# Image keys of batches 3 to 10 of a cross-attention: two batches at a time, by seven products for eight blocks, with the context sums on VectorE

## The chip, the core and the metric

The kernel runs on one core of a Trainium2 chip. The metric is the device time of one execution in microseconds (us); lower is better. Engines are named as the profile names them: PE is TensorE (PEld its weight loads), DVE is VectorE, ACT is ScalarE, POOL is GpSimd, SP is SyncE. ACT and SP also issue DMAs.

## The reference

Input `x` is 16 batches of 512 tokens by 640 channels, the context `ctx_2048` 16 batches of 512 tokens by 1024 channels. Context tokens 0 to 76 are text, then come 4 object and 4 other tokens, and 427 image tokens. Cut to what matters (`heads` splits 640 channels into 20 heads of 32):

```python
q = heads(x @ to_q_w)
h_txt = sdpa(q, heads(txt @ to_k_w), heads(txt @ to_v_w))
h_obj = sdpa(q, heads(obj @ to_k_object_w), heads(obj @ to_v_object_w))
h_oth = sdpa(q, heads(oth @ to_k_others_w), heads(oth @ to_v_others_w))
h_ip  = sdpa(q, heads(ip @ to_k_ip_w), heads(ip @ to_v_ip_w))
out = (h_txt + h_obj + h_oth + h_ip) @ to_out_w + to_out_b + x
```

The change is in `ip @ to_k_ip_w`, the image keys: for each batch a product of 427 tokens, 1024 input channels and 640 output channels.

## The kernel before

All is float32. A product is made from operands in two parts, a high one (`fp32r`) and the rest, by three passes: high by high, high by low, low by high. To **split** an operand, ACT copies the raw numbers into the high part (`split_hi`), then DVE takes the difference raw minus high into the low part (`split_lo`).

The program has two stages. The first makes keys and values of the whole context, the second is attention. The first goes by one list, `ORDER`: text keys (`("k", run, m)` with run 0 to 3), text values (`"v"`), values of the other tokens (`"g"`, which already makes seven products for eight), and then the image keys, runs 4 to 19 for batches 0 to 15. The **step** `("k", run, m)` is block `m` of 5 blocks of 128 output channels: 8 chunks of 128 input channels by 3 passes, 24 matmuls of 428 columns. Two short steps `("s", 2, 0)` and `("s", 3, 0)` make the values of the object and other tokens; they read `w_small` and write through `t_ps`. Each engine walks `ORDER` in its own instruction stream, and waits only on semaphores:

- PE makes the block. The bank it writes must have been read by the two engines below (`k_lo`).
- ACT does at each step, in this order: the high parts that `SPLITS` puts there, the high part of the finished block into `k_out` (`keep_k`), and then the DMAs that **store** the block of the step before (`store_k`), which wait for DVE (`k_lo`) and for POOL's copy of 8 small columns (`k_fill`). `k_out` has 4 places in turn.
- DVE does the low parts that `SPLITS` puts there and then the low part of the finished block.

The context of a batch is split during the five steps of the batch before it, 8 pieces of 128x428, two by two:

```python
for run in range(TXT + 1, RUNS):
    spread("c", K_LOAD[run], ("k", run - 1, 1), (2, 2, 2, 2))
```

From batch 12 on the first queries and scores of attention are mixed into the list (`FIRST_...`). In the profile, tensor names are cut: PSUM banks are `s_ps`, `st_ps` and `om_ps` (they share memory with `v_ps`, `k_ps` and `t_ps`).

Of the kernel before, what the change touches and what calls it, by code (L numbers as in the profile page):

```python
# [14 lines left out]
BATCH = 16  # L15
# [4 lines left out]
P = 128  # L20
# [37 lines left out]
OP_PARTS = ((B11, B22), (B22, T4), (T4, OPS))  # L58
V_TILES = 3
# [840 lines left out]
def project_context(nc, d):  # L900
# [63 lines left out]

    w, w_raw = {"k_txt": w0, "v_txt": w2}, {"k_txt": w0_raw, "v_txt": w2_raw}
# [21 lines left out]
    sv_stored = sem("sv_stored")  # L987
    d["late"] = LateKeys(w_ip, c0, k_late, k_stored, k_fill)
# [16 lines left out]
    def landed(load):  # L1005
        return 16 * sum(buffer(n) == buffer(load) for n in range(load + 1))
# [161 lines left out]
    def sync_part(sp):  # L1168
        def load_c(load, n):
            run, b = LOAD_RUN[load], buffer(load)  # L1170
            rows = slice(n * P, (n + 1) * P)
            if n == 0:
                if 2 <= load < TXT:
                    sp.wait_ge(k_acc, k_base(load - 1))
                elif TXT <= load < TXT + 2:
                    sp.wait_ge(v_acc, v_base[V_TXT[load - TXT + 1]])
                elif TXT + 2 <= load < TXT + 4:
                    sp.wait_ge(g_acc, OPS * (TILE_PAIRS - 1 + load - TXT - 2))
                elif load >= TXT + 4:
# [88 lines left out]
        for b in range(2, BATCH - 1):  # L1268
            for n in range(CC):
                load_c(K_LOAD[TXT + b], n)  # L1270
            if b == 2:
                for n in range(CC):
                    load_halves("v", 1, n)
            if b == 4:
                store_late_small()
            if b == 5:
                sp.wait_ge(s_acc, 4)
                sp.wait_ge(sv_stored, 32)
                for n in range(QC):
                    sp.dma_start(wq_raw[:, n, :], d["wq"][n * P:(n + 1) * P, :]).then_inc(wq_in[n], 16)  # L1280
                    sp.dma_start(x_raw[:, n, :], d["xT"][0, n * P:(n + 1) * P, :]).then_inc(x_in[n], 16)
# [23 lines left out]
    def scalar_part(act):  # L1305
        def split_hi(kind, which, n):
# [33 lines left out]
        def keep_k(run, m):  # L1340
            k0, (to, at, n) = k_base(run) + m, k_cols(run)
# [88 lines left out]
        def keep(step):  # L1430
# [40 lines left out]
    def vector_part(dve):  # L1471
        def split_lo(kind, which, n):
# [22 lines left out]
        def weight_sums():  # L1495
# [9 lines left out]
            dve.wait_ge(a_sum, 4)  # L1505

# [85 lines left out]
    def gpsimd_part(pool):  # L1592
        def fill_small(run, m):

            k0, b = k_base(run) + m, run - TXT
# [6 lines left out]
        for run in range(TXT, RUNS):  # L1602
            for m in k_slots(run):
                fill_small(run, m)
                if (run, m) in FIRST_LESS:
                    first.less_max(*FIRST_LESS[(run, m)])
# [7 lines left out]
    def tensor_part(pe):  # L1614
# [31 lines left out]
        def k_block(run, m):  # L1646
# [8 lines left out]
            for q in range(CC):  # L1655
# [86 lines left out]
        for kind, a, b in ORDER:  # L1742
# [110 lines left out]
```

## Time and profile before

| | us |
|---|---|
| median of 3 runs | 2382.55 (2382.27 to 2383.14) |
| the profiled execution | 2382.65 |
| its span in the profile | 2380.4 |
| image keys of batches 0 to 11, with the two `"s"` steps, in it | 489.44 to 812.32 |

The span is what the profiler saw between the first and the last instruction; 2.25 us of the execution lie around it. "Busy" is the time in which an engine has an instruction under way; DMA issues are listed under ACTq and SPq and don't count as busy.

### The profile page before, as it was taken

The page shows a single profiled execution, that of the slowest core. Times are in us where ns is not written, and L with a number is a line of the kernel's source. Part 1 is how long each engine was busy: PE and PEld are TensorE (multiplying, and loading weights), DVE is VectorE, ACT ScalarE, POOL GpSimd, SP SyncE. Part 2 cuts the span into 40 slices and gives each one's busy share as a digit, 9 for nine tenths or more (in the row PEclk, how much of TensorE's full clock was granted, in tenths as well). Part 3 has the DMA queues.
Part 4 walks back from the last instruction along what each step waited for, and adds up shares of the span by engine and source line. Part 5 has one row for each costly group of instructions (what it writes and reads, how often), then busy time and mean ns, then how long its engine had stood idle before and what let it go on. Part 6 is the DMA issues. An engine that isn't in the chain of part 4 may idle for free.

```text
span 2380.4 us, 37663 instructions
## 1 busy us (share of the span) xinstructions
PE 2366.0 (99%) x12801; PEld 1802.3 (76%) x12801; DVE 1834.2 (77%) x3291; ACT 1776.6 (75%) x3906; POOL 413.0 (17%) x564
## 2 busy tenths in 40 slices
PE   9999999999999999999999999999999999999999
PEld 8999999998999986566666666666666666666665
DVE  3457777732333489999999999999999999999994
ACT  4343433322223369999999999999999999999995
POOL 0000000000000023413223133133132231231310
PEclk9999999999999999999999999999999999999999
DMA  9545444374644555546555556555556555565542
GB/s 338 162 129 159 150 136 141 109 268 147 233 167 174 182 174 153 148 129 154 150 145 146 133 147 159 138 147 151 128 157 151 137 150 140 144 161 129 147 132 78
DMA packets 371749, 370.12 MB, mean 155 GB/s; under 512 B 110046, under 2 KB 298590, under 8 KB 371558
## 3 DMA queue, kind: packets, MB, share of 16 engines
q1 hardware_dynamic: 334384, 306.14, 47.5%
q10 hardware_dynamic: 37174, 61.59, 7.0%
q8 instruction: 101, 1.65, 0.3%
q14 instruction: 90, 0.74, 0.1%
HBM read 215.57 MB, written 83.89 MB: 126 GB/s over the span
## 4 chain that ended last, share of the span: by engine, by line
PE 97%; ACT 2%; issue 0%; DMA 0%; DVE 0%; ACTq 0%
PE st_ps L1660 17%; PE s_ps L489 13%; PE st_ps L509 12%; PE om_ps L523 12%; PE om_ps L544 11%; PE om_ps L567 11%; PE s_ps L1712 7%; PE om_ps L1712 4%; PE s_ps L1680 3%; PE st_ps L1712 3%; ACT s_ps L689 1%; PE om_ps L1729 1%; ACT probs L681 1%; PE om_ps L602 1%; PE st_ps L1620 0%
## 5 line engine op out<-in xcount | busy, mean ns | idle before, releaser
L689 ACT ACTIVATE s_ps<-s_ps,negmax 128x427 f32<-128x427 f32 x1280 | 768.4, 609 | 21.5 <-DVE small L758 21.5
L749 DVE TENSOR_REDUCE negmax<-s_ps 128x2 f32<-128x854 f32 x640 | 665.2, 1039 | 77.3 <-PE s_ps L489 71.1
L681 ACT ACTIVATE probs<-st_ps 128x1024 f32<-128x1024 f32 x632 | 656.4, 1039 | 15.3 <-PE st_ps L509 3.7
L489 PE MATMUL s_ps<-kpack,qpack 96*128 96x512 f32 x1280 | 420.8, 410 | 2.1 <-ACT s_ps L689 2.1
L509 PE MATMUL st_ps<-qpack,kpack 104*128 104x512 f32 x1264 | 404.9, 401 | 3.2 <-ACT probs L681 3.1
L447 POOL TENSOR_TENSOR small<-small,negmax 128x616 f32<-128x616 f32 x160 | 196.6, 1229 | 999.6 <-DVE negmax L766 999.5
L1660 PE MATMUL st_ps<-ctx_split,w_split_ip 128*128 128x428 f32 x1848 | 364.2, 357 | 0.0
L1660 PEld LDWEIGHTS st_ps<-ctx_split,w_split_ip 128*128 128x128 f32 x1848 | 347.0, 188 | 15.6 <-issue 1.0
L489 PEld LDWEIGHTS s_ps<-kpack,qpack 96*128 96x128 f32 x1280 | 222.9, 189 | 178.2 <-ACT s_ps L689 81.2
L544 PE MATMUL om_ps<-xs,wq 128*128 128x512 f32 x1200 | 340.1, 393 | 0.0
L567 PE MATMUL om_ps<-heads,wo 128*128 128x512 f32 x1125 | 320.8, 393 | 0.0
L523 PE MATMUL om_ps<-probs,vt 128*32 128x512 f32 x2560 | 308.6, 598 | 0.8 <-ACT probs L681 0.7
L689 ACT ACTIVATION_READ_ACCUMULATOR s_ps<-s_ps,negmax 128x1 f32 x1280 | 290.4, 227 | 0.0
L509 PEld LDWEIGHTS st_ps<-qpack,kpack 104*128 104x128 f32 x1264 | 214.5, 189 | 94.4 <-ACT probs L681 35.3
L544 PEld LDWEIGHTS om_ps<-xs,wq 128*128 128x128 f32 x1200 | 226.0, 188 | 54.2 <-DVE out L839 0.5
L567 PEld LDWEIGHTS om_ps<-heads,wo 128*128 128x128 f32 x1125 | 212.0, 188 | 50.6 <-DVE heads L827 2.7
L1525 DVE TENSOR_TENSOR k_out<-st_ps,k_out 128x427 fp32r<-128x427 f32 (+2 forms) x94 | 54.2, 577 | 231.6 <-ACT k_out L1348 231.5
L1348 ACT ACTIVATE k_out<-st_ps 128x427 fp32r<-128x427 f32 (+2 forms) x94 | 47.7, 508 | 235.7 <-PE st_ps L1660 227.7
L758 DVE COPY small<-s_ps 128x170 f32<-128x170 f32 x640 | 207.2, 324 | 0.0
L523 PEld LDWEIGHTS om_ps<-probs,vt 128*32 128x32 f32 x2560 | 66.4, 109 | 154.1 <-issue 152.6
L1712 PE MATMUL s_ps<-w_ops,tok_ops 128*128 128x320 f32 (+1 forms) x1176 | 174.8, 309 | 0.0
L1712 PEld LDWEIGHTS s_ps<-w_ops,tok_ops 128*128 128x128 f32 (+1 forms) x1176 | 173.0, 185 | 0.0
(116 smaller groups left out, 2437.0 us busy)
## 6 DMA issues: line engine op xcount, KB each, us to landing
qpack<-q_out SPq DMA_DIRECT2D x240, 256.0 KB, 4.8
kpack<-kT SPq DMA_DIRECT2D x240, 217.5 KB, 3.0
kT<-k_out ACTq DMA_DIRECT2D x154, 217.5 KB, 3.2
ctx_split_raw<-in_ctxT SPq DMA_DIRECT2D x128, 214.0 KB, 4.5
tok_pair<-in_ctxT SPq DMA_DIRECT2D x48, 512.0 KB, 4.7
xs_raw<-in_xT SPq DMA_DIRECT2D x85, 256.0 KB, 4.0
out<-in_xT SPq DMA_DIRECT2D x75, 256.0 KB, 4.2
out_yT<-out SPq DMA_DIRECT2D x75, 256.0 KB, 2.1
```

The costliest lines, as they stand in the source:

```text
L447: nc.gpsimd.tensor_tensor(txt, txt, over_keys(m_txt, N_TXT), ALU.add).then_inc(sm_sub, 1)
L489: last = nc.tensor.matmul(s_ps[:, n % 2, z, :], qpack[r][0:ROWS_S, j, t * P:(t + 1) * P], kpack[r][0:ROWS_S, j, :], start=True, stop=True)
L509: last = nc.tensor.matmul(transposed(u, duo)[:, z, :], kpack[r][0:ROWS_ST, j, kt * P:(kt + 1) * P], qpack[r][0:ROWS_ST, j, :], start=True, ...
L523: last = nc.tensor.matmul(o_ps[j * HD:(j + 1) * HD, :], vt[r][:, kt, j * HD:(j + 1) * HD], probs[:, (ITEMS * u + HPU * kt + j) % PR, :], s ...
L544: last = nc.tensor.matmul(m_ps[:, :], wq[:, pw, c, cols], xs[:, px, c, :], start=(n == 0), stop=(n == PRODUCTS - 1))
L567: last = nc.tensor.matmul(m_ps[:, :], wo[:, pw, z, cols], heads[:, (w // QC * QC + z) % HR, po, :], start=(n == 0), stop=(n == PRODUCTS - 1))
L681: nc.scalar.activation(probs[:, at:at + 2, :], transposed(u, duo), ACT.Exp).then_inc(p_done, 1)
L689: last = nc.scalar.activation(s_ps[:, n % 2, z, SMALL:TOK], s_ps[:, n % 2, z, SMALL:TOK], ACT.Exp, bias=negmax[:, r, IP, j, t:t + 1], accu ...
L749: nc.vector.tensor_reduce(negmax[:, r, IP, j, t0:t0 + 2], s_ps[:, n % 2, :, SMALL:TOK], AX_X, ALU.max, negate=True).then_inc(s_max, 1)
L758: nc.vector.tensor_copy(small[:, w:w + 2, :], s_ps[:, n % 2, :, 0:SMALL]).then_inc(s_max, 1)
L1660: last = nc.tensor.matmul(k_place(run, m)[:, 0:n], weights, c[b][:, px, q, a:a + n], start=(q == 0 and z == 0), stop=(q == CC - 1 and z == ...
L1712: last = nc.tensor.matmul(pair_bank(g, i), ops[r][:, px, i, q, 0:rows], w_ops[:, pw, i, q, :], start=not adds and q == 0 and z == 0, stop= ...
```

## The change

Batches 3 to 10 are made as four **pairs** (`K_PAIRS`). Blocks 0 to 3 of both batches are one product of 2 by 2 by 2 parts (2 batches, 2 halves of the input channels, 2 halves of 512 output channels), made by seven products instead of eight. Block 4 of each is made as before. A pair is 18 **groups** (`K_GROUPS`) of 12 matmuls of 428 columns, in place of 10 blocks of 24. The step is `("p", pair, i)` for group i.

The moving operands are eight, z0 to z7 (`K_OPERANDS`): half a batch's channels (128x1712 numbers), or a sum of such (T3, T2, T4, T1, made by `key_sum` on DVE). All eight are split, each into one of three slots of `k_ops`. The weight sums S1 to S4 are made once, during batch 2 (`key_weight_sums`, split as `"sw"`). Parts of results are combined on DVE (`add_group`), ten additions of 128x428 a pair; ACT copies two (`keep_x`). Blocks come out at groups 7 to 15 and 17, and are kept and stored as before. PE waits for some of the additions (`u_add`), for groups 14 and 15 for those behind groups 12 and 13. The steps `"s"` stand one batch sooner.

```diff
+K_PAIRS = ((3, 4), (5, 6), (7, 8), (9, 10))
+K_OPERANDS = (B11, T3, T2, T4, B21, T1, B22, "B12")
+K_SLOTS = 3
+K_GROUPS = ((0, "X", 0), (0, "X", 1), (0, "F", 0), (1, "Q", 0), (1, "Q", 1), (2, "U", 0), (2, "U", 1),
+            (3, "Q", 0), (3, "Q", 1), (4, "X", 0), (4, "X", 1), (4, "F", 0), (5, "U", 0), (5, "U", 1),
+            (6, "U", 0), (6, "U", 1), (6, "F", 1), (7, "F", 1))
+K_OUT = {7: (0, 2), 8: (0, 3), 9: (0, 0), 10: (0, 1), 11: (0, 4), 12: (1, 2), 13: (1, 3), 14: (1, 0), 15: (1, 1), 17: (1, 4)}
...
-        ORDER += [("k", run, m) for m in k_slots(run)]
-        ORDER += {TXT + 1: [("s", 2, 0)], TXT + 2: [("s", 3, 0)]}.get(run, [])
+        if run - TXT not in K_PAIRED:
+            ORDER += [("k", run, m) for m in k_slots(run)]
+        elif K_PAIRED.index(run - TXT) % 2 == 0:
+            ORDER += [("p", K_PAIRED.index(run - TXT) // 2, i) for i in range(len(K_GROUPS))]
+        ORDER += {TXT: [("s", 2, 0)], TXT + 1: [("s", 3, 0)]}.get(run, [])
...
+        if run == behind_pairs:
+            spread("c", K_LOAD[run], ("p", len(K_PAIRS) - 1, 14), (2, 2, 2, 2))
...
+    for pp in range(len(K_PAIRS)):
+        ahead = [("k", before_pairs, 3), ("k", before_pairs, 4)] if pp == 0 else [("p", pp - 1, 15), ("p", pp - 1, 17)]
+        for j, step in enumerate(ahead + [("p", pp, i) for i in (0, 3, 6, 9, 11, 13)]):
+            SPLITS.setdefault(step, []).append(("z", pp, j))
+    T_SUMS = {}
+    for pp in range(len(K_PAIRS)):
+        ahead = [("k", before_pairs, 3), ("k", before_pairs, 4)] if pp == 0 else [("p", pp - 1, 10), ("p", pp - 1, 16)]
+        for i, step in zip((T3, T2, T4, T1), ahead + [("p", pp, 3), ("p", pp, 7)]):
+            T_SUMS[step] = (i, pp)
...
+        def keep_group(pp, i):
+            run, m = pair_block(pp, i)
+            k0, (to, at, n) = k_num(run, m), k_cols(run)
+            _, kind, t = K_GROUPS[i]
+            if kind in "QU":
+                act.wait_ge(u_add, U_ADDS * pp + {7: 5, 8: 6, 12: 7, 13: 8, 14: 9, 15: 10}[i])
+            else:
+                act.wait_ge(k_acc, k0 + 1)
+            act.wait_ge(k_stored[k0 % KR], stored_upto(k0 % KR, k0))
+            src = u3_k[:, t, :] if i in (12, 13) else bank(pp, kind, t)
+            nc.scalar.activation(k_out[:, k0 % KR, HI, to:to + n], src[:, at:at + n], ACT.Copy).then_inc(k_hi, 1)
...
+        def add_group(pp, i):
+            if i in (5, 6):
...
+                nc.vector.tensor_tensor(u2, bank(pp, "U", t), u2, ALU.add).then_inc(u_add, 1)
+                dve.wait_ge(u_add, n + 2 * t + 1)
+                nc.vector.tensor_tensor(u3, bank(pp, "Q", t), u2, ALU.add).then_inc(u_add, 1)
...
+            elif i in (12, 13):
+                dve.wait_ge(k_acc, k_num(*pair_block(pp, i)) + 1)
+                dve.wait_ge(u_add, n + 4)
+                nc.vector.tensor_tensor(u3, bank(pp, kind, t), u3, ALU.add).then_inc(u_add, 1)
...
             if step in SUMS:
+            if step in T_SUMS:
+                key_sum(*T_SUMS[step])
             for piece in SPLITS.get(step, ()):
                 split_lo(*piece)
...
+            elif kind == "p":
+                add_group(a, b)
+                if b - 1 in K_OUT:
+                    keep_group(a, b - 1)
+                if b == len(K_GROUPS) - 1:
+                    keep_group(a, b)
...
+        def k_group(pp, i):
+            j, kind, t = K_GROUPS[i]
+            base, z = pair_base(pp), z_number(pp, j)
+            if i == 0 or K_GROUPS[i - 1][0] != j:
+                pe.wait_ge(piece_lo, split_upto(("z", pp, j)))
...
+            elif i in (7, 8):
+                pe.wait_ge(u_add, U_ADDS * pp + 2 * (t + 1))
+            elif i in (9, 10):
+                pe.wait_ge(u_add, U_ADDS * pp + 2 * t + 1)
+            elif i in (14, 15):
+                pe.wait_ge(u_add, U_ADDS * pp + 7 + t)
...
+            for q in range(CC2):
+                for n, (pw, px) in enumerate(PASSES):
```

On ACT a step is walked as before: high parts of `SPLITS`, keep (here `keep_x` or `keep_group`), store of the step before.

DVE's stream in the middle of a batch, before the change. L1493 is the low part of a context piece, L1525 the low part of a finished block:

```order
L1525 TENSOR_TENSOR k_out<-st_ps,k_out 128x427 x2
L1493 TENSOR_TENSOR ctx_split_83<-ctx_split_raw,ctx_split_83 128x428 x2
L1525 TENSOR_TENSOR k_out<-st_ps,k_out 128x427
L1493 TENSOR_TENSOR ctx_split_83<-ctx_split_raw,ctx_split_83 128x428 x2
L1525 TENSOR_TENSOR k_out<-st_ps,k_out 128x427
L1493 TENSOR_TENSOR ctx_split_83<-ctx_split_raw,ctx_split_83 128x428 x2
L1525 TENSOR_TENSOR k_out<-st_ps,k_out 128x427
```

DVE's stream from step 8 of pair 1 on, after the change. L1670 is the low part of an operand (`k_ops`), L1710 a context sum (`t_raw`; here T3 of pair 2), L1746 and L1742 additions (of groups 12, 13 and 14), L1754 the low part of a block; the first row keeps group 7, the second splits z5:

```order
L1670 TENSOR_TENSOR k_ops_114<-k_ops_raw,k_ops_114 128x1712
L1754 TENSOR_TENSOR k_out<-s_ps,k_out 128x427
L1710 TENSOR_TENSOR t_raw<-ctx_raw_110 128x1712
L1754 TENSOR_TENSOR k_out<-s_ps,k_out 128x427
L1670 TENSOR_TENSOR k_ops_116<-ctx_raw_111,k_ops_116 128x1712
L1754 TENSOR_TENSOR k_out<-s_ps,k_out 128x427
L1746 TENSOR_TENSOR u_k<-om_ps,u_k 128x428
L1754 TENSOR_TENSOR k_out<-st_ps,k_out 128x427
L1670 TENSOR_TENSOR k_ops_112<-ctx_raw_111,k_ops_112 128x1712
L1746 TENSOR_TENSOR u_k<-om_ps,u_k 128x428
L1754 TENSOR_TENSOR k_out<-u_k,k_out 128x427
L1742 TENSOR_TENSOR om_ps<-om_ps,u_k 128x428
```

So between two blocks DVE now has an operand of 1712 columns to split or to sum, and the addition of group 12 stands behind z6, that of group 13 behind z7.

ACT's stream in the middle of a batch before, where L1322 is the high part of a context piece, L1348 that of a block, L1363 its stores:

```order
L1322 ACTIVATE ctx_split_81<-ctx_split_raw 128x428 x2
L1348 ACTIVATE k_out<-st_ps 128x427
L1363 DMA kT<-k_out 128x435 x2
L1322 ACTIVATE ctx_split_81<-ctx_split_raw 128x428 x2
L1348 ACTIVATE k_out<-st_ps 128x427
L1363 DMA kT<-k_out 128x435 x2
L1322 ACTIVATE ctx_split_81<-ctx_split_raw 128x428 x2
L1348 ACTIVATE k_out<-st_ps 128x427
L1363 DMA kT<-k_out 128x435 x2
```

and in pair 1 after, from the stores of group 7 on (L1464 is the high part of an operand, L1509 that of a block, L1524 its stores):

```order
L1524 DMA kT<-k_out 128x435 x2
L1464 ACTIVATE k_ops_114<-k_ops_raw 128x1712
L1509 ACTIVATE k_out<-s_ps 128x427
L1524 DMA kT<-k_out 128x435 x2
L1509 ACTIVATE k_out<-s_ps 128x427
L1524 DMA kT<-k_out 128x435 x2
L1464 ACTIVATE k_ops_116<-ctx_raw_111 128x1712
L1509 ACTIVATE k_out<-st_ps 128x427
L1524 DMA kT<-k_out 128x435 x2
L1509 ACTIVATE k_out<-u_k 128x427
L1524 DMA kT<-k_out 128x435 x2
L1464 ACTIVATE k_ops_112<-ctx_raw_111 128x1712
```

The stores of a block (L1524) now stand directly ahead of an operand's high part (L1464) three times in these rows, and wait for DVE's low part of that block.

## Rows read from the trace of the kernel before

**Rows 1.** The page: busy time by engine; busy tenths and granted clock of PE.

```profile
span 2380.4 us, 37663 instructions
...
PE 2366.0 (99%) x12801; PEld 1802.3 (76%) x12801; DVE 1834.2 (77%) x3291; ACT 1776.6 (75%) x3906; POOL 413.0 (17%) x564
...
PE   9999999999999999999999999999999999999999
...
PEclk9999999999999999999999999999999999999999
```

**Rows 2.** Chain that ended last, 480 to 815 us: start, us, what.

```profile
489.44 46.80 PE st_ps L1660 x240
536.24 4.46 PE om_ps L1729 x32
540.70 23.60 PE st_ps L1660 x120
564.30 4.46 PE om_ps L1729 x32
568.75 243.56 PE st_ps L1660 x1248
```

**Rows 3.** Windows view: busy us (instructions) of PE, PEld, DVE, ACT, POOL; clock; DMA.

```profile
568.75:812.32 243.57, 243.57 (x1250) 234.69 (x1250) 83.57 (x143) 74.75 (x144) 10.09 (x51) 1.00 0.54 185
```

**Rows 4.** Timeline, one step of batch 5: start, us, engine, what.

```profile
620.47 0.53 ACT L1348 ACTIVATE k_out<-st_ps 128x427 fp32r<-128x427 f32 x1 [4.15 <-PE st_ps L1660]
620.53 0.81 ACTq L1363 DMA_DIRECT2D kT<-k_out  x2
621.03 0.60 DVE L1525 TENSOR_TENSOR k_out<-st_ps,k_out 128x427 fp32r<-128x427 f32 x1 [4.08 <-ACT k_out L1348]
621.06 0.20 POOL L1598 CAST k_out<-k_small 128x16 fp32r<-128x16 f32 x1 [4.48 <-ACT k_out L1348]
621.39 1.01 ACT L1322 ACTIVATE ctx_split<-ctx_split_raw 128x428 fp32r<-128x428 f32 x2 [0.39 <-POOL k_out L1598]
621.99 1.12 DVE L1493 TENSOR_TENSOR ctx_split<-ctx_split_raw,ctx_split 128x428 fp32r<-128x428 f32 x2 [0.35 <-ACT ctx_split L1322]
625.15 0.53 ACT L1348 ACTIVATE k_out<-st_ps 128x427 fp32r<-128x427 f32 x1 [2.75 <-PE st_ps L1660]
```

**Rows 5.** Groups by line and form, 120 to 475 us.

```profile
L1493 DVE TENSOR_TENSOR tok_ops<-tok_ops_raw,tok_ops 128x2048 fp32r<-128x2048 f32 x26 | 59.3, 2281 | 0.3 <-ACT tok_ops L1338 0.3
L1338 ACT ACTIVATE tok_ops<-tok_ops_raw 128x2048 fp32r<-128x2048 f32 x26 | 49.5, 1903 | 0.0
...
L1546 DVE TENSOR_TENSOR v_out<-om_ps,u_part 128x320 f32<-128x320 f32 x13 | 6.4, 492 | 1.6 <-PE om_ps L1712 0.5
...
L1493 DVE TENSOR_TENSOR tok_ops<-tok_ops_raw,tok_ops 128x1408 fp32r<-128x1408 f32 x1 | 1.6, 1626 | 0.3 <-ACT tok_ops L1338 0.3
L1338 ACT ACTIVATE tok_ops<-tok_ops_raw 128x1408 fp32r<-128x1408 f32 x1 | 1.4, 1362 | 0.0
```

**Rows 6.** Timeline at a change of bank in the values' products.

```profile
439.86 3.56 PEld L1712 LDWEIGHTS st_ps<-w_ops,tok_ops 128*128 128x128 f32 x24
440.00 3.68 PE L1712 MATMUL st_ps<-w_ops,tok_ops 128*128 128x320 f32 x24
...
440.20 0.49 DVE L1551 TENSOR_TENSOR v_out<-s_ps,u_part 128x320 f32<-128x320 f32 x1 [1.27 <-PE s_ps L1712]
440.61 0.68 DVE L1514 TENSOR_TENSOR tok_ops_raw<-tok_pair 128x512 f32<-128x512 f32 x1
441.21 0.68 DVE L1515 TENSOR_TENSOR tok_ops_raw<-tok_pair 128x512 f32<-128x512 f32 x1
```

**Rows 7.** Timeline at the start, where stores follow blocks closely.

```profile
26.80 1.10 DVE L1525 TENSOR_TENSOR k_out<-st_ps,k_out 128x385 fp32r<-128x385 f32 x2 [6.24 <-ACT k_out L1348]
...
27.39 0.82 ACTq L1363 DMA_DIRECT2D kT_txt<-k_out  x2
...
28.26 0.49 ACT L1348 ACTIVATE k_out<-om_ps 128x385 fp32r<-128x385 f32 x1 [0.96 <-DVE k_out L1525]
28.29 1.17 ACTq L1363 DMA_DIRECT2D kT_txt<-k_out  x2
...
29.54 2.40 ACTq L1363 DMA_DIRECT2D kT_txt<-k_out  x2
```

**Rows 8.** Timeline of SP's queue: last load of the first half.

```profile
505.96 0.51 SPq L1205 DMA_DIRECT2D w_small<-in_v_oth  x1
```

**Rows 9.** The tile w_small: landing of its loads.

```profile
DMA to landing us min/median/max: 2.6/4.7/6.7
```

**Rows 10.** The tile kT: ns of one issue, least/median/most.

```profile
L1363 ACTq DMA_DIRECT2D kT<-k_out x154: 326/359/1107, 498.9 to 878.9; - x154
```

**Rows 11.** Groups by line, first 20 us: PE's wait there.

```profile
L1620 PE MATMUL st_ps<-ctx_split,w_split 128*128 128x386 f32 x30 | 7.4, 382 | 4.9 <-ACT ctx_split L1322 4.9
```

More of the change, by code:

```diff
@@ L58 @@
 OP_PARTS = ((B11, B22), (B22, T4), (T4, OPS))
+K_PAIRS = ((3, 4), (5, 6), (7, 8), (9, 10))
+K_PAIRED = tuple(b for pair in K_PAIRS for b in pair)
+K_OPERANDS = (B11, T3, T2, T4, B21, T1, B22, "B12")
[4 more added lines that the diff above has]
+K_OUT = {7: (0, 2), 8: (0, 3), 9: (0, 0), 10: (0, 1), 11: (0, 4), 12: (1, 2), 13: (1, 3), 14: (1, 0), 15: (1, 1), 17: (1, 4)}
+K_OUT_ORDER = tuple(K_OUT.values())
+U_ADDS = 10
+S_PARTS = (S1, S2, S3, S4)
 V_TILES = 3
@@ L1005, in landed @@
     def landed(load):
-        return 16 * sum(buffer(n) == buffer(load) for n in range(load + 1))
+        return 16 * sum(buffer(n) == buffer(load) and LOAD_RUN[n] - TXT not in K_PAIRED for n in range(load + 1))
     def is_txt(run):
@@ L1042, in k_base, with k_num @@
         return run * QC
+    def k_num(run, m):
+        b = run - TXT
+        if b not in K_PAIRED:
+            return k_base(run) + m
+        first, second = K_PAIRS[K_PAIRED.index(b) // 2]
+        return k_base(TXT + first) + K_OUT_ORDER.index((b - first, m))
     K_ALL = k_base(RUNS) - DEFER
@@ new lines, in z_raw, with bank @@
+    def z_raw(pp, j):
+        i, (b11, b21, b12, b22) = K_OPERANDS[j], (raw[pp % 2][:, h, k, :, :] for h in range(2) for k in range(2))
+        in_slot = slots_raw[z_number(pp, j) % K_SLOTS][:, LO, :, :]
+        return {B11: b11, B21: b21, B22: b22, "B12": b12, T3: t3_raw[:, :, :], T2: t2_raw[:, :, :], T4: in_slot, T1: in_slot}[i]
+    def bank(pp, kind, t):
+        if kind == "F":
+            return k_ps[:, (pair_base(pp) + K_OUT_ORDER.index((t, QC - 1))) % 2, 0:IPN]
+        if kind == "U":
+            return t_ps[:, t, 0:IPN]
+        return v_ps[:, "XQ".index(kind), t, 0:IPN]
@@ L1507, in token_sums, with keep_group @@
+        def keep_group(pp, i):
+            run, m = pair_block(pp, i)
+            k0, (to, at, n) = k_num(run, m), k_cols(run)
+            _, kind, t = K_GROUPS[i]
+            src = u3_k[:, t, :] if i in (12, 13) else bank(pp, kind, t)
+            dve.wait_ge(k_hi, k0 + 1)
+            nc.vector.tensor_tensor(k_out[:, k0 % KR, LO, to:to + n], src[:, at:at + n],
+                                    k_out[:, k0 % KR, HI, to:to + n].bitcast(F32), ALU.subtract).then_inc(k_lo, 1)
         def token_sums(g):
@@ L1593, in fill_small @@
         def fill_small(run, m):
[L1595 removed]
+            k0, b = k_num(run, m), run - TXT
             pool.wait_ge(k_hi, k0 + 1)
@@ L1601, in gpsimd_part @@
         first = att.pool_ops(pool)
[L1602 to L1606, printed above, removed]
+        for step in ORDER[ORDER.index(("k", TXT, 0)):]:
+            kind, a, b = step
+            if kind == "k":
+                fill_small(a, b)
+                if (a, b) in FIRST_LESS:
+                    first.less_max(*FIRST_LESS[(a, b)])
+            elif kind == "p" and b in K_OUT:
+                fill_small(*pair_block(a, b))
         pool.wait_ge(k_acc, K_ALL)
```

209 lines of the change are left out of this document (199 added, 10 removed).

## The prediction

> **What bounds the kernel now.** The page comes first: PE is busy for 99% of the span, in every slice, at the full granted clock of 2.4 GHz [rows 1]. Then the chain that ended last, in the stretch that the change touches: one uninterrupted line of PE, 1248 matmuls of the image keys in 243.56 us, with nothing in between [rows 2]. That is 0.1952 us a matmul, 4.68 us a block of 24, 2.34 us a group of 12. DVE works for 84 of these 243.6 us and ACT for 75 [rows 3], so the engines that feed PE have room, and by busy time alone fewer matmuls are shorter time. What the reader must still see is how the two feeders hang together, and that stands in the timeline of one step [rows 4]: ACT keeps a block, its two stores hold ACT's stream for 0.81 us and its next work starts 0.05 us later, DVE starts 0.03 us behind the instruction of ACT that it waits for. That is some 2 us of hand-overs in a step of 4.68 us, and PE never notices.
>
> **What is removed.** A pair needs 18 x 12 = 216 matmuls, before 10 x 24 = 240. Four pairs save 96, by 0.1952 us 18.7 us, since shape and passes are the same [rows 2]. This is the whole gain; nothing else is taken from PE.
>
> **What is added.** Prices for 428 and 1712 columns. A low part or a sum of 1712 numbers on DVE: between 1408 at 1.626 and 2048 at 2.281, so 1.94. Its high part on ACT: between 1.362 and 1.903, so 1.62 [rows 5]. An addition of 428 that reads PSUM: 0.49 at 320 [rows 5], and 427 columns with PSUM take 0.60 [rows 4], so 0.60. Each DVE instruction that waits for nothing starts 0.08 before the end of the one ahead (0.60 apart at 0.68 long) [rows 6]: in a row they cost 1.86 and 0.52. DVE or ACT starts 0.20 us after PE has gone on to the next bank; PE's weight load leads its matmul by 0.14 [rows 6], and I take 0.20 from DVE to PE too. For hand-overs between ACT and DVE I take 0.04.
>
> DVE's work in a pair: 8 low parts and 4 sums, 23.3 us, 10 additions and 10 low parts of blocks, 12.0 us, together 35.3. PE's is 216 x 0.1952 = 42.2. ACT's is 8 x 1.62 + 12 x 0.53 + 10 x 0.81 = 27.4. So each fits under PE. But they wait for each other in the order of their streams, and the second half of a pair is one chain. I follow it from PE's last matmul of group 8, time 0:
>
> - DVE adds group 8 (0.20 + 0.60), keeps 7 (0.52): 1.32. ACT stores 7, which waits for that (0.04 + 0.86): 2.22. Only then its stream comes to z5: high part 1.62, 3.84; low part on DVE 1.97, 5.81.
> - DVE keeps 8 (0.52), makes T3 of the next pair (1.86), keeps 9 (0.52): 8.72. ACT stores 9 (0.90): 9.62, high part of z6: 11.24, low part: 13.21.
> - DVE keeps 10 (0.52), adds group 12 (0.52): 14.25; PE may start group 14 at 14.45. Groups 9 to 13 last 5 x 2.34 = 11.71. **PE stands for 2.7 us.**
> - From the end of that addition: DVE keeps 11 (0.52), ACT stores 11 (0.90), high part of z7 (1.62), low part (1.97), DVE adds group 13 (0.52), 0.20 to PE: 5.74. PE is back after 0.20 + 2.34 = 2.54. **It stands for 3.2 us** ahead of group 15. z7 is wanted only at group 17, but its low part stands ahead of the addition in DVE's stream.
> - From the addition of group 13 to the second addition behind group 6 of the next pair, the same way (low parts of z0 to z4, T2, T4, nine short ones, and stores 13 and 15 and four high parts that DVE waits for): 26.2 us with the step to PE, against 0.20 + 11 x 2.34 = 26.0. **0.3 us**.
>
> That stores ahead of ACT's work really hold it, the start of the kernel shows: low parts finish, the stores issue at 27.39 for 0.82 us, and ACT's next block, ready long before, begins at 28.26 [rows 7].
>
> The first pair stands 2.7 + 3.2 = 5.9 us (its z0 and z1 are made during batch 2). Pairs 1 and 2 stand 6.2 each. The last has no T3 ahead of z6; 1.86 less would leave 0.9, but ACT's own keeps and stores then come last, by my count at 1.3; with 0.3 and 3.2 that is 4.8. Behind it batch 11 can't begin before group 15 is kept. From the addition of group 13, three rounds of keep 0.52, store 0.90, two high parts 1.03, the low part behind 0.70 and an addition or keep 0.52 make 11.0, and with 0.2 to PE 11.2, where PE needs 0.2 + 3 x 2.34 = 7.2: 4.0 us. **Sum of the waits: 5.9 + 12.4 + 4.8 + 4.0 = 27.1 us.**
>
> What costs nothing: the weight sums (four of 1024 columns, about 1.2 us each, and their splits) lie in batch 2, which has no pieces of the next batch to split any more. POOL's 0.20 us copies run beside DVE's low part [rows 4]. `"s"` 2 moves to 512.8 (489.44 + 23.4); its last load was issued at 505.96 [rows 8], and such loads land after 4.7 us, 6.7 at most [rows 9], so by 511.2 or 513.2: 0 to 0.4 us. Contexts of the pairs are the same bytes in larger loads and are asked for half a pair ahead.
>
> **Sum:** -18.7 + 27.1 = +8.4 us. On the profiled 2382.65 this is 2391.1; the median of the runs is 0.1 lower, so **2391.0 us**, slower by 0.35%.
>
> **Bounds of the unknowns.** No row has stores this dense: two every 2.34 us, beside loads of 3.5 MB. The nearest rows are 0.81 us, and where stores followed each other closely 1.17 and 2.40 for two [rows 7]. With 1.17 each chain is longer by 0.36 a store (pairs have three up to group 15 and two behind, the end has three), some 9 us: 2400. If stores held ACT for nothing, the waits would be 1.1 + 2.4 in a pair, 1.7 in the last and 1.6 at the end, 13.8 in all: 2378. A hand-over of 0.10 in place of 0.04 is worth 3 us, 1.87 in place of 1.94 for 1712 columns -2 us. I take 0.81: of 154 issues of such stores the median is 0.36 and only the longest 1.11 [rows 10], and two with the gap between them are the 0.81 of [rows 4].
>
> **Rivals.**
>
> *It hides (faster).* The one mechanism is the same chain, shorter: if stores and high parts of one step could overlap so far that the walk from group 8 to group 14 stays under 11.7 us and that from 14 to 15 under 2.5, PE would run through: 2382.55 - 18.7 = 2363.8. For it speaks the sum of busy time, 35 of 42 us on DVE, and that the values' products already run in sevens with PE never idle [rows 1]. Against it: it decides when the waits fall under 18.7 of 27.1 us, and even free stores leave 13.8, which gives 2377.6. Chance 0.10, with times from 2364 to 2378.
>
> *It cancels (no change).* Waits of 14 to 23.5 us: stores of about 0.4 to 0.6 us in the chain, or my order wrong at one of its two long places (the wait ahead of group 14 alone is 9.5 us in four pairs). 2378 to 2387, chance 0.16.
>
> *The clock falls too.* In the chain above PE stands twice within 8 us, for 2.7 and 3.2. In the kernel before it stands for 4.9 us in the first 20 [rows 11] and no slice has less than the full clock [rows 1]. Were the groups behind a stop made at the lower level, 1.2 GHz, each would take up to twice 2.34 us; one group in each of five stops is 12 us more, 2403. Chance 0.08. The Trainium skill, "TensorE: Matmul & The Clock Gate", Why this matters for your kernels, says that idle gaps between bursts bring the array back to half its clock, and its section on oscillation describes kernels that pay this at each tile. By this rule the time would be near that of this rival; the trace doesn't bear it out at the one long stop that it has.
>
> *Stores or loads collide.* Stores of 1.17 us and more, or a place of `k_out` that is free late: 2397 to 2405, chance 0.08.
>
> The forecast itself has 0.58, and its own range is 2387.5 to 2397.
>
> **How the numbers follow.** 0.2% is 4.8 us, about what a measurement of this kernel tells from no change. Slower: forecast, clock and collision, 0.58 + 0.08 + 0.08 = 0.74; same 0.16; faster 0.10. The range that leaves out the faster case, a quarter of the cancelling one and half of the two dear ones goes from 2380 to 2402.
>
> **What would show it.** In the windows of the pairs PE works 42.2 us of some 48 in each, in stops directly ahead of groups 14 and 15, put down to DVE's additions of groups 12 and 13 (L1746 of the new kernel); ACT's high parts of z5, z6 and z7 wait for DVE's low part of a block (L1754) or for nothing but the stores' issue; and a stop of about 4 us at the start of batch 11. Granted clock 1.00 throughout. If PE runs through the pairs, stores don't hold ACT as in [rows 7]. If the stops lie ahead of groups 0 or 3, loads or z0 and z1 are late, which I have as done. What would make the prediction wrong above all is the price of a store in ACT's stream, then the hand-overs.

## The result and the profile after

The changed kernel takes 2397.7 us (median of 4 runs, 2395.2 to 2398.3), against 2382.6 before: slower by 0.61% (ratio 1.0061, 95% interval 1.0049 to 1.0074), 15.1 us. The forecast was 2391.0, range 2380 to 2402, slower. So sign and range held, but of the 15.1 us the central sum had 8.4, and 2397.7 lies just outside the forecast's own range of 2387.5 to 2397. In a second series of four runs it took 2397.9 (2395.1 to 2399.4). The profiled execution took 2395.2, with a span of 2393.4.

The page of the changed kernel, for [rows 1]:

```profile
span 2393.4 us, 37555 instructions
...
PE 2358.0 (99%) x12705; PEld 1792.8 (75%) x12705; DVE 1918.1 (80%) x3323; ACT 1801.7 (75%) x3886; POOL 432.9 (18%) x564
...
PE   9999999999889999999999999999999999999999
...
PEclk9999999999999999999999999999999999999999
```

PE has 96 matmuls fewer and 8 us less to do, and two slices of the 40 show 8 tenths where there was a 9. The tenths of the clock are too coarse to show what follows. The next rows are PE's part of the timeline over the four pairs, only with the pieces before which PE stood or which last too long. A row gives start us, us, what, and in brackets the wait. A group of 12 at full clock is listed with 2.6 us, since the end of its last matmul is counted in; for the same reason a listed wait is some 0.2 us shorter than the stop in the forecast's sum.

```profile
604.43 2.58 PE L1970 MATMUL om_ps<-k_ops,s_weights 128*128 128x428 f32 x12 [2.59 <-DVE u_k L1746]
609.93 4.16 PE L1970 MATMUL om_ps<-k_ops,s_weights 128*128 128x428 f32 x12 [2.92 <-DVE u_k L1746]
613.93 4.85 PE L1970 MATMUL st_ps<-k_ops,w_split_ip 128*128 128x428 f32 x24
...
654.17 4.12 PE L1970 MATMUL om_ps<-k_ops,s_weights 128*128 128x428 f32 x12 [2.58 <-DVE u_k L1746]
659.92 2.60 PE L1970 MATMUL om_ps<-k_ops,s_weights 128*128 128x428 f32 x12 [1.63 <-DVE u_k L1746]
...
675.05 4.96 PE L1970 MATMUL s_ps<-k_ops,s_weights 128*128 128x428 f32 x24 [0.81 <-DVE k_ops L1670]
...
704.76 3.95 PE L1970 MATMUL om_ps<-k_ops,s_weights 128*128 128x428 f32 x12 [3.30 <-DVE u_k L1746]
710.27 2.60 PE L1970 MATMUL om_ps<-k_ops,s_weights 128*128 128x428 f32 x12 [1.56 <-DVE u_k L1746]
...
752.28 2.58 PE L1970 MATMUL om_ps<-k_ops,s_weights 128*128 128x428 f32 x12 [1.51 <-DVE u_k L1746]
757.78 4.65 PE L1970 MATMUL om_ps<-k_ops,s_weights 128*128 128x428 f32 x12 [2.93 <-DVE u_k L1746]
762.23 5.46 PE L1970 MATMUL st_ps<-k_ops,w_split_ip 128*128 128x428 f32 x24
768.67 11.58 PE L1923 MATMUL st_ps<-ctx_split,w_split_ip 128*128 128x428 f32 x58 [0.98 <-DVE k_out L1754]
```

In each pair PE stands ahead of group 14 (604.43, 654.17, 704.76, 752.28) and group 15 (609.93, 659.92, 710.27, 757.78), each time for the addition of group 12 or 13 (L1746). And in each pair there is one group, in the last more than one, that lasts about 4 us or more. The windows view of the four pairs, each up to the next one's first matmul, the last up to batch 11 (columns as in [rows 3]):

```profile
568.87:618.62 49.75, 44.23 (x218) 41.89 (x216) 30.92 (x31) 17.49 (x19) 5.75 (x10) 0.97 0.55 185
618.62:667.06 48.44, 44.23 (x218) 41.87 (x216) 31.87 (x32) 18.58 (x20) 6.72 (x10) 0.96 0.43 153
667.06:717.38 50.32, 44.56 (x217) 41.34 (x216) 33.55 (x34) 19.08 (x21) 7.81 (x10) 0.97 0.46 164
717.38:768.67 51.29, 45.79 (x218) 42.51 (x217) 33.35 (x38) 20.26 (x26) 7.82 (x11) 0.93 0.39 140
```

Lengths are 49.75, 48.44, 50.32 and 51.29 us, for 42.2 us of matmuls each, and the clock is 0.93 to 0.97 where it was 1.00 [rows 3]. So 199.8 us go by for 168.7 of matmuls: 31.1 are lost and 18.7 saved, which makes it 12.4 dearer. The profiled executions differ by 12.6. Below, a sum "by lengths" is this one, from group 0 of pair 0 to batch 11 less the matmuls; it holds the slow groups too, which the listed waits don't.

The chain of the forecast can be read in the timeline of pair 1, from the stores of group 7 on, without PE (ACT and DVE only; for the step before, see [rows 4]):

```profile
641.05 0.81 ACTq L1524 DMA_DIRECT2D kT<-k_out  x2
...
641.96 1.63 ACT L1464 ACTIVATE k_ops<-k_ops_raw 128x1712 fp32r<-128x1712 f32 x1 [0.88 <-POOL k_out L1858]
...
643.63 1.94 DVE L1670 TENSOR_TENSOR k_ops<-k_ops_raw,k_ops 128x1712 fp32r<-128x1712 f32 x1 [2.61 <-ACT k_ops L1464]
...
645.49 0.60 DVE L1754 TENSOR_TENSOR k_out<-s_ps,k_out 128x427 fp32r<-128x427 f32 x1
646.00 1.93 DVE L1710 TENSOR_TENSOR t_raw<-ctx_raw 128x1712 f32<-128x1712 f32 x1
...
647.85 0.60 DVE L1754 TENSOR_TENSOR k_out<-s_ps,k_out 128x427 fp32r<-128x427 f32 x1
648.48 0.81 ACTq L1524 DMA_DIRECT2D kT<-k_out  x2
...
651.06 1.95 DVE L1670 TENSOR_TENSOR k_ops<-ctx_raw,k_ops 128x1712 fp32r<-128x1712 f32 x1 [2.61 <-ACT k_ops L1464]
...
652.92 0.60 DVE L1754 TENSOR_TENSOR k_out<-s_ps,k_out 128x427 fp32r<-128x427 f32 x1
653.43 0.60 DVE L1746 TENSOR_TENSOR u_k<-om_ps,u_k 128x428 f32<-128x428 f32 x1
```

Store (641.05), high part of z5 (641.96), low part (643.63), block kept (645.49), T3 (646.00), block kept (647.85), store (648.48), high part of z6 behind it, low part (651.06), block kept, and only at 653.43 the addition that PE waits for. In this list nothing overlaps the next by more than 0.1 us.

### The profile page after: what moved, and what is told of

The parts are those of the page before. It is cut to its first block, busy times and chain, and to the rows that moved or that the text cites. A ratio compares the mean times of both kernels' runs of the same rounds, so it can differ in the third digit from the quotient of the medians.

```text
span 2393.4 us, 37555 instructions
## 1 busy us (share of the span) xinstructions
PE 2358.0 (99%) x12705; PEld 1792.8 (75%) x12705; DVE 1918.1 (80%) x3323; ACT 1801.7 (75%) x3886; POOL 432.9 (18%) x564
## 4 chain that ended last, share of the span: by engine, by line
PE 91%; ACT 3%; DVE 2%; issue 2%; ACTq 1%; DMA 0%; DVEq 0%
PE s_ps L500 13%; PE st_ps L520 12%; PE om_ps L534 12%; PE om_ps L555 11%; PE om_ps L578 11%; PE st_ps L1923 9%; PE s_ps L2024 7%; PE om_ps L2024 4%; PE s_ps L1992 3%; PE st_ps L2024 3%; PE s_ps L1970 1%; ACT k_ops L1464 1%; ACT s_ps L700 1%; ACTq L1524 1%; PE om_ps L2041 1%
## 5 line engine op out<-in xcount | busy, mean ns | idle before, releaser
L520 PEld LDWEIGHTS st_ps<-qpack,kpack 104*128 104x128 f32 x1264 | 216.0, 189 | 91.6 <-ACT probs L692 28.7
L1858 POOL CAST k_out<-k_small 128x16 fp32r<-128x16 f32 x77 | 36.0, 467 | 835.9 <-ACT k_out L1490 662.7
L1923 PE MATMUL st_ps<-ctx_split,w_split_ip 128*128 128x428 f32 x888 | 177.3, 358 | 1.0 <-DVE k_out L1754 1.0
L1923 PEld LDWEIGHTS st_ps<-ctx_split,w_split_ip 128*128 128x128 f32 x888 | 166.8, 188 | 9.8 <-DVE k_out L1754 1.3
L708 ACT ACTIVATE small<-small 128x680 f32<-128x680 f32 x160 | 130.0, 813 | 0.0
```

Of the source, the lines that this page charges most:

```text
L520: last = nc.tensor.matmul(transposed(u, duo)[:, z, :], kpack[r][0:ROWS_ST, j, kt * P:(kt + 1) * P], qpack[r][0:ROWS_ST, j, :], start=True, ...
L1923: last = nc.tensor.matmul(k_place(run, m)[:, 0:n], weights, c[b][:, px, q, a:a + n], start=(q == 0 and z == 0), stop=(q == CC - 1 and z == ...
```

## The experiments

**e1: stores of the pairs issued by SP.**

```diff
-            elif kind == "p":
-                if b in K_OUT:
-                    store_k(*pair_block(a, b))
...
+        def store_group(pp, i):
+            sp.wait_ge(k_lo, k0 + 1)
+            sp.wait_ge(k_fill, k0 - k_base(TXT) + 1)
...
+        for pp in range(2):
+            for i in K_OUT:
+                store_group(pp, i)
+            load_raw(pp + 2)
```

> The changed kernel, but the 40 stores of the pairs' blocks are issued by SP instead of ACT. Theory of the chain (the forecast's): PE's stops come from ACT's and DVE's streams waiting for each other, with each store's wait and issue (0.9 us) ahead of a high part on ACT. Without them the same count leaves 6 us of stops, some 1.4 ahead of group 15 in each pair and about 1 at batch 11, so 2382.6 - 18.7 + 6.4 = 2370, and with stops this short the granted clock stays at 1.00. Rival, DVE simply has too much work in a pair (its instructions are the same here): the stops stay, 2395 to 2398.

Measured 2371.1 us (2369.7 to 2372.3), ratio 0.9950 (0.9935 to 0.9964). PE's waits in the pairs and at batch 11 (engine, what, us in total, times, longest):

```profile
PE om_ps L1983 <- DVE u_k L1759: 3.8, 4, 1.1
PE st_ps L1936 <- DVE k_out L1767: 0.8, 1, 0.8
```

PE stands 1.1 ahead of group 15 and 0.6 in the last pair, 0.8 at batch 11, and not at all ahead of group 14, at clock 1.00. By lengths 5.9 us are lost, where the count had 6. DVE's instructions are the same, so a DVE with too much work is out. (SP now issues the loads of pairs 2 and 3 behind the stores of pairs 0 and 1, as the edit shows; PE never waits for them.)

**e2: DVE's additions first.** `add_group` is called ahead of `key_sum` and `split_lo`.

> The changed kernel, but in each step of a pair DVE's addition stands ahead of the operand's sum and low part. Theory of the chain: the stop of 3.2 us ahead of group 15 goes, since the addition of group 13 no longer stands behind z7; but the low parts of blocks come later, so PE waits some 1.7 us ahead of group 16 for kept blocks, and group 14 waits 3.5 instead of 2.7; in sum 24 instead of 27 us of stops: 2393 to 2396. Rival, the stops are a matter of how much DVE has to do: no change, 2397.7, with the stops where they were. If only the stop at group 15 counted: 2385.

Measured 2395.9 us (2394.7 to 2396.7), some 2 us less than the changed kernel, with runs that overlap. PE's waits:

```profile
PE om_ps L1971 <- DVE u_k L1746: 12.1, 4, 3.4
PE st_ps L1924 <- DVE k_out L1754: 5.3, 1, 5.3
PE s_ps L1971 <- DVE k_ops L1670: 4.2, 4, 2.4
```

The stops ahead of group 15 are gone, those ahead of 14 are 3.3 to 3.4 (2.2 in the last pair), as expected. The wait for kept blocks that I expected ahead of group 16 does not show; what shows is z0 late, up to 2.4 us ahead of the next pair's group 0, and 5.3 at batch 11. By lengths 28.7 us are lost instead of 31.1, where the count had 3 less. The loop takes back elsewhere what the one stop gives: right in sum, wrong in place.

**e3: POOL's small copies early.** `fill_small` waits for `k_stored` in place of `k_hi`.

> The changed kernel, but POOL's copy of the 8 small columns waits only for the place in k_out to be free, not for ACT's high part, so that it is long done when the store wants it. In the trace of the changed kernel 40 of these copies last up to 1.78 us instead of 0.20, ending with a DVE instruction of 1712 columns. Theory that this holds the stores of group 14 and so z1: the wait of 0.8 us ahead of group 3 goes and the times fall by 1 to 3 us, to 2395 to 2396.5. Rival, the stores wait for DVE's low part of the block at least as long everywhere that matters: no change, 2397.7. The stops ahead of 14 and 15 stay under both.

Measured 2397.4 us (2395.2 to 2398.7): no change, the rival. The wait ahead of group 3 of pair 2 is still there, 1.0 us. In the changed kernel 17 of the 40 copies are long ones, and each of them ends some 0.45 us before the low part that the same store also waits for (669.25 and 669.70 in pair 2).

**e4: stops filled with matmuls that nobody reads.**

```diff
+            if i in (14, 15):
+                pe.wait_ge(k_lo, base + 2)
+                for n in range(FILL[i] if (i, pp) != (14, len(K_PAIRS) - 1) else 7):
+                    nc.tensor.matmul(v_ps[:, 1, 0, 0:3 * P], s_w[:, S_PARTS.index(S4), HI, n % CC2, 0:P],
+                                     w_ip[:, 0, HI, 0:3, :], start=True, stop=True)
```

> The changed kernel, but PE fills its stops ahead of groups 14 and 15 with 13 and 15 matmuls of 384 columns (7 in the last pair's first), 2.3 and 2.7 us, whose result nobody reads. They add to PE's work nothing that the stops would not hide. Theory of the clock: groups made at the half clock behind the stops (the four marked by 4.0 to 4.7 us instead of 2.6) cost what the forecast missed; here the granted clock is 1.00 throughout, and the time falls by 3 to 5 us, to 2393 to 2395. Rival, a slow group is hidden in the next stop, since the next addition is late anyway: clock 1.00 but only some 0 to 2 us won, 2396 to 2398, and the forecast's error lies in the chain.

Measured 2396.1 us (2394.7 to 2398.7); the profile fell on 2398.7. In it pair 0 runs from 568.50 to 616.70, 48.2 us in place of 49.75, with full clock: so the slow group of pair 0 did cost 1.6 us. But in pair 1 one store took 2.56 us for its two issues, z7 came late, PE stood 2.3 us behind its filling and the clock fell there. That pair took 52.4 us for 48.4, and the clock fell again at batch 11 and at the opening of attention, so 1.00 throughout, which the theory had, did not come. The gain of the medians, 1.6 us, is within the spread. The granted clock of all runs says more than the one profile: 0.998 to 0.999 in the four of e4, 0.994 to 0.996 in the eight of the changed kernel, and still the times overlap. So a large part of the falls was gone and little time came back. That favours the rival: the clock's share in the pairs is small.

**e5: e1 and e2 together.**

> Both edits together: stores of the pairs' blocks issued by SP, and DVE's additions ahead of sums and low parts. Theory of the chain: with ACT's stream free of stores the chain from group 8 to group 14 is shorter than PE's work, and the addition of group 13 no longer stands behind z7; the count leaves no stop at all, the whole saving of 18.7 us stays: 2364 (up to 2366 with the 1 to 2 us that run e1 lost beside its stops), clock 1.00. Rival, DVE's 35 of 42 us leave too little room and each order has its stops: 2370 or more, like the first edit alone.

Measured 2365.5 us (2364.1 to 2366.9), ratio 0.9927 (0.9912 to 0.9942), faster than the kernel before by 17 us and than the changed one by 32. The windows view over 168.7 us, the time of 864 matmuls (the pairs themselves run from 569.60 to 738.34):

```profile
569.00:737.70 168.70, 168.70 (x865) 162.49 (x865) 130.16 (x132) 75.03 (x86) 30.38 (x40) 1.00 0.51 178
```

PE is busy for all 168.7 us at clock 1.00, and no wait of PE is listed in the pairs. DVE is busy for 130 of them, 77%, and is not the bound.

**e6: T3 four steps later** (`[("p", pp - 1, 14), ("p", pp - 1, 16)]`).

> The changed kernel, but T3 of the next pair is made on DVE at step 14 instead of step 10, so 1.86 us less stands ahead of z6. Theory of the chain: ACT and DVE are one loop around the pair, as long as before, so the time moves only from one stop to others: ahead of group 14 about 1.3 instead of 2.7, but new stops of 0.9 ahead of group 16 and of group 3: in sum 28.3 us of stops instead of 27.1, time 2397 to 2400. Rival, each stop has a cause of its own and this one is cut at its cause: three times 1.4 us less, 2393.5. Rival of the clock: the stops get shorter and the clock falls less often, 2393 or less.

Measured 2397.5 us (2395.7 to 2400.3): no gain. Ahead of group 14 PE stood 1.3, 1.2, 2.2 and 1.5 us in place of 2.6, 2.6, 3.3 and 1.5, but 0.8 ahead of group 0 of pair 1 and 0.5 to 1.1 ahead of group 3 of three pairs. None stands ahead of group 16, where I had expected one of 0.9. By lengths 32.3 us are lost for 31.1. What is taken from one stop turns up in the next: the loop is the bound, not a place.

**e7: two pairs** (`K_PAIRS = ((3, 4), (5, 6))`).

> Only batches 3 to 6 as pairs, 7 to 10 as before. This gives the price of one inner pair and that of entering and leaving. By the forecast's count: saving 9.4 us, stops 5.9 + 4.8 + 4.0 = 14.7, so +5.3 us: 2388; by the changed kernel's trace, where each pair's loop was some 1 to 2 us dearer and the clock fell, 2389 to 2392. The two pairs left out would then be worth +3 (count) to +7 us. Rival, the loss is a single event at the way out and the pairs themselves gain: more than 2398.

Measured 2391.5 us (2390.8 to 2391.8), ratio 1.0036 (1.0022 to 1.0049): +8.6 over the kernel before in the same series (2382.9), where the count said +5.3. It lies in the 2389 to 2392 that I had from the changed kernel's trace. With four pairs it is +14.9 in that series (e8), so an inner pair loses 3.2 us where the count had 1.5.

**e8: the changed kernel again.**

> The changed kernel unaltered, once more, for its spread: its four runs lay between 2395.2 and 2398.3, those of the kernel before within 1 us. In the profiles of e3 and e4 the clock also fell at about 899 us, at the opening of attention, where the changed kernel's first profile (2395.2) has 1.00. If this is what the spread is, a profiled run of 2397.5 or more has the fall at about 899 or a long wait at batch 11 at full clock, one of 2395 has neither. If not, profiles at both times look alike there.

Measured 2397.9 us (2395.1 to 2399.4), the profiled run 2396.8. It has no fall at the opening of attention, but its clock is low in every pair and for ten us in the third, pair 2. It lies between the two cases that I named and shows only that the place of a fall varies.

**e9: stores on ACT one step later.**

```diff
-            if i > 0:
+            if i > 1 and ORDER[i - 2][0] == "p":
+                store(ORDER[i - 2])
+            if i > 0 and ORDER[i - 1][0] != "p":
                 store(ORDER[i - 1])
```

> The changed kernel, but ACT issues the stores of a pair's block two steps behind the block instead of one. The same 80 issues stay in ACT's stream; only the wait for DVE's low part of the block is over when ACT comes to them. Theory that it is the wait, a turn of the loop between ACT and DVE, and not the issue that counts: the stops ahead of group 14 go, 2.2 us ahead of group 15 and 2.6 at batch 11 are left, 11.3 in all, so 2375 to 2378. Rival, the issue itself (0.81 us each) holds ACT: the stops stay near 24 to 27, 2393 to 2397.

Measured 2379.2 us (2375.9 to 2379.9, 10 runs), ratio 0.9984 (0.9974 to 0.9993).

```profile
PE om_ps L1972 <- DVE u_k L1748: 8.3, 4, 2.2
PE st_ps L1925 <- DVE k_out L1756: 2.3, 1, 2.3
```

PE stands 1.9 to 2.2 ahead of each group 15, 2.3 at batch 11, and not at all ahead of group 14, which is the count. The median is 1.2 us above the range that I gave, since the clock still fell: group 15 of pair 0 took 4.15 us, and the profile has a fall at the opening of attention too, some 1.6 us each. All 80 issues are still in ACT's stream, so most of what a store costs is the wait for DVE ahead of the next high part. By lengths 13.3 us are lost here, 17.8 less than in the changed kernel, and 5.9 with the issues out of ACT's stream too (e1).

**e10: one DMA a store.**

> The changed kernel, but each stored block is one DMA of both parts instead of two (in all blocks, those before the pairs too). The wait for DVE stays ahead of the high parts, the issue is half as long. By the forecast's count the stops are 19.8 instead of 27.1 us, all still ahead of groups 14 and 15 and at batch 11: 2389 to 2392. If the issue is not on the loop at all: 2397. If one DMA of two parts takes as long to issue as two: 2397.

Measured 2386.6 us (2384.4 to 2387.5, 10 runs), ratio 1.0016 (1.0007 to 1.0026). PE stands 1.7 ahead of group 14 (not in the last pair) and 2.5 ahead of group 15; with batch 11 the listed waits make 17.1 us. By lengths 22.2 are lost, 8.9 less than in the changed kernel, where the count had 7.3 less, and the time is 2.4 us below the range that I gave. The issues, least/median/most ns, of the changed kernel and of this one:

```profile
L1524 ACTq DMA_DIRECT2D kT<-k_out x154: 321/454/1587, 499.0 to 891.9; - x154
```

```profile
L1523 ACTq DMA_DIRECT2D kT<-k_out x77: 361/366/415, 498.7 to 882.1; - x77
```

A store of both parts in one DMA issues in 0.37 us and never in more than 0.42. With two, the median over all issues says little, 0.45 against 0.36 [rows 10]: issue by issue the trace has 0.33 for the first and 0.46 for the second both in the kernel before and in the changed one (medians). What differs is the longest, 1.59 against 1.11, and in both it is a second one.

**e11: e9 and e2 together.**

> Stores two steps behind on ACT, and DVE's additions first. By the count 0.1 us is left ahead of group 14, 0.8 us ahead of group 16 in three pairs, and 1.5 at batch 11, 4.5 in all: 2368 to 2371, against 2365.5 with the stores on SP. If the issues on ACT matter more than the count has them, 2375 and more.

Measured 2369.8 us (2369.2 to 2370.6), ratio 0.9947 (0.9932 to 0.9962), clock 1.00.

```profile
PE s_ps L1973 <- DVE k_ops L1672: 2.4, 3, 1.1
PE st_ps L1926 <- DVE k_out L1756: 1.2, 1, 1.2
```

By lengths 5.3 us are lost, against 4.5 in the count. The size is as expected, the place is not: PE stands 0.6 to 1.1 ahead of group 0 of three pairs, for z0, and not ahead of group 16. The time is 4 us behind e5.

## Why the prediction was right, and where it was short

**What bounds the kernel, and the saving.** This was right. 864 matmuls of pairs take 168.7 us in e5, the 0.1952 us of [rows 2], and e5, at 2365.5 for 2382.6, keeps 17.1 of the 18.7 us saved.

**Prices.** A low part of 1712 columns took 1.94, its high part 1.63, an addition 0.60, the hand-overs between ACT and DVE 0.03 to 0.04. From DVE to PE they were 0.05 to 0.15, where I took 0.20.

**The chain.** It was right in kind and places, and the experiments leave no other: shortened on ACT's side (e1, e9, e10) it gives 11 to 27 us back, shifted (e6) nothing, reordered on DVE's side alone (e2) some 2, within the spread, and with both sides done (e5) PE never stops. By pair, measured over the forecast's (lengths less 42.2): 7.6 for 5.9, 6.3 for 6.2, 8.2 for 6.2, and 9.1 for 4.8 + 4.0.

**What was too small.** The sum of stops has 27.1 where 31.1 were lost in the profiled run. Two terms make up most of this: the clock, which I had at nothing (1.6 in pair 0), and the stores (2.0, with what hangs on them, in pair 2). A third part, the 2.5 us from the profiled run to the median, is not in the sum at all.

- *The clock*, which I had as a rival with 0.08. It fell in every pair. Here it is in pair 0, behind the two stops:

```profile
604.40:606.00 1.60, 1.57 (x8) 1.54 (x9) 0.39 (x1) 0.80 (x2) 0.20 (x1) 1.00 0.85 307
...
608.00:609.90 1.90, 0.00 (x0) 0.00 (x0) 1.90 (x3) 0.00 (x0) 0.00 (x0) 1.00 0.00 0
609.90:611.00 1.10, 1.06 (x3) 1.02 (x4) 1.10 (x3) 0.56 (x1) 0.20 (x1) 0.54 0.20 42
611.00:612.00 1.00, 1.00 (x4) 0.93 (x4) 0.41 (x1) 0.43 (x1) 0.00 (x0) 0.50 0.79 235
612.00:613.00 1.00, 1.00 (x5) 0.93 (x4) 0.00 (x0) 0.31 (x2) 0.20 (x1) 0.50 0.97 318
...
614.00:615.00 1.00, 1.00 (x7) 0.97 (x6) 0.55 (x1) 0.42 (x1) 0.00 (x0) 1.00 0.76 224
```

  Group 15 ran at the lower level, 1.2 GHz, for some 3.5 us, which cost 1.6 us. But in the other pairs the slow group mostly cost nothing: in pair 1 group 14 was the slow one (4.12 us), and the stop ahead of 15 shrank to 1.6, since PE would have waited for z7 anyway. In the last pair slow groups ate most of the 4.0 us at batch 11, of which only 1.0 is listed. e3 shows that this was free up to batch 11: there the last pair ran at full clock, PE stood 3.6 us at batch 11, and the pair took 51.26 us against 51.29. My price of 12 us left that cover out. The Trainium skill, "TensorE: Matmul & The Clock Gate", Why this matters for your kernels, has the fall behind idle gaps: by that rule, the trace agrees in each pair. Shorter gaps than its table names were enough here, down to 1.9 us (e9), and others as long had no fall. The stop of [rows 11], my one witness against it, is the time before PE's first matmul of all, so there was no work ahead of it that it could have interrupted:

```profile
4.94 1.01 PE L1620 MATMUL st_ps<-ctx_split,w_split 128*128 128x386 f32 x2 [4.94 <-ACT ctx_split L1322]
```

- *Stores.* I priced them at 0.81 for two throughout. In pair 2:

```profile
667.38 3.90 ACTq L1524 DMA_DIRECT2D kT<-k_out  x4
667.47 1.78 POOL L1858 CAST k_out<-k_small 128x16 fp32r<-128x16 f32 x1 [5.08 <-ACT k_out L1509]
669.11 0.59 DVE L1754 TENSOR_TENSOR k_out<-om_ps,k_out 128x427 fp32r<-128x427 f32 x1
671.38 1.64 ACT L1464 ACTIVATE k_ops<-t_raw 128x1712 fp32r<-128x1712 f32 x1 [3.97 <-issue]
```

  The 3.90 us hold two stores of two issues each, and the wait between them. The first store takes 0.81. The second waits for DVE's low part, which stands behind the sum and ends at 669.70, and then takes 1.54. A second such store comes ahead of z5's high part in the same pair:

```profile
669.74 1.54 ACTq L1524 DMA_DIRECT2D kT<-k_out  x2
...
690.92 1.52 ACTq L1524 DMA_DIRECT2D kT<-k_out  x2
```

  So each is 0.7 us dearer than my 0.81. Behind the first PE stood 0.8 ahead of group 3, behind the other 3.3 ahead of group 14 instead of 2.6. The loads of 3.5 MB are under way at this time, 396 GB/s from 667 to 671. e10 with one DMA a store has no such issue; why an issue takes longer is open. POOL's copy of 0.20 us takes 1.78 in the same rows, up to the end of DVE's sum, and I put part of the delay on it; e3 took this away and won nothing.
- *Outside the pairs*, for the median. The profiled run is the lower end of the runs. In e3's profile (2398.7) the clock falls once more at the opening of attention, in the changed kernel's (2395.2) it does not:

```profile
880.00:905.00 25.00, 23.78 (x103) 20.19 (x102) 20.24 (x39) 17.27 (x46) 10.73 (x12) 0.93 0.83 219
```

```profile
880.00:905.00 25.00, 23.78 (x112) 20.55 (x112) 20.10 (x39) 19.24 (x50) 10.73 (x12) 1.00 0.83 222
```

  Of the 13 profiled executions of this study, six have such a fall: e3, e4, e5, e6, e9 and e10. The first four are the highest run of their kernel (2398.7, 2398.7, 2366.9, 2400.3), the last two are not. The stops there are the same in all 13, 0.35 and 0.84 us, the kernel before included, so why the clock falls in some executions only is open. From e3 against the changed kernel I read its price: from the first of these stops to the last image key it took 49.9 us for 48.3, so 1.6, and from batch 11 to that stop, with one more fall at batch 11, 128.9 for 127.4, again some 1.6. The granted clock of the single runs supports this where PE hardly stops: e5 has 1.000 in its runs of 2364.1 and 2364.8 and 0.999 in those of 2366.2 and 2366.9, and of the 19 runs of the kernel before only the two highest (2383.1, 2383.5) have 0.999. The changed kernel's runs, 0.994 to 0.996, don't line up with their times, so for it this is likely, not shown.

**What I took to cost nothing** did cost nothing: the step `"s"` 2 began at 512.91 without a wait, and the weight sums hid in batch 2, which lasted 23.60 us as before.

**The rivals.** "It hides" was wrong for this kernel, and right for e5: busy time had the room, the order of the streams did not. I had bounded the case of free stores at 2378; with SP they came to 2371, because they then also cease to wait in ACT's stream. The bound priced only the issue, and e9 shows that the wait is the larger part: by lengths 17.8 us for the wait, another 7.4 for the issues themselves (e1). The parts don't simply add: with the wait in place, half the issue was worth 8.9 (e10). The clock and the dearer stores, which I had apart with 0.08 each, both came, at 1.6 and 2.0 us in the profiled pairs instead of 12 and some 9. (The 9 us themselves are too many: by my own count of stores, five in each of three pairs and three each in the last pair and behind it, 0.36 us a store makes 7.6.)

## What to carry to other kernels

When an engine with 99% busy time is given less work, add up not only the busy time of those that feed it but the longest walk from one engine to the other in the order of their streams; a DMA issue that waits for another engine is a turn in that walk, and moving it to an idle queue or one step later was worth 18 to 27 us here. Moving work about within one stream of such a loop (e2, e6) only moves the stop; taking a turn out of it, or making every turn shorter (e10), shortens the loop. Put what the bound engine waits for ahead of work that is wanted later.

## What the runs showed of the hardware

- One stop of PE can be enough for the granted clock to fall to 0.50. It fell behind listed stops from 1.9 us (e9, pair 0) to 3.5 (e8, pair 2), with no other stop near, and stayed low for some 3.5 us, in the last pair of the changed kernel for some 7, in that pair of e8 for ten. It did not fall behind others of the same size (2.2 in e9, 3.3 in the first pair of e2), nor behind those of 1.1 and 1.2 us in e1 and e11. At the opening of attention two stops of 0.35 and 0.84 us, 1.6 us apart, had the fall in six of 13 executions.
- A POOL copy of 128x16 that starts beside a DVE `tensor_tensor` with both inputs in SBUF lasts until that instruction ends: mostly 1.55 to 1.78 us for 0.20. The Trainium skill, "SBUF — State Buffer", Who interferes with whom, says that a DVE instruction with two SBUF inputs contends with a GpSimd instruction that reads SBUF; the trace agrees.
- Two DMA issues, 0.81 us in ACT's stream, took up to 2.56 (e4), one DMA with the same bytes 0.36 to 0.42 at all times (e10).
